# One-hot rows with two steps side by side, and two kinds of products taken in turn, in a graph network stack

## The chip, the cores and the metric

The kernel runs on one core of one Trainium2 chip. The metric is the device time of one execution in microseconds; the kernel before is shown with the median of three runs.

## What is computed

Four graph layers (GCN, graph attention with edge attributes, two GAT convolutions, two SAGE convolutions) run one after another over 3125 nodes with 128 features and 50000 edges. The edges come sorted by their target `dst`. Around each layer there is a layer norm with a relu, and a residual:

```python
edge_index = jnp.stack([src, dst])
h = jnp.maximum(_layernorm(x, axis=-1), 0.0)
x = x + _L0_gnn_ref(h, L0_gnn_W, L0_gnn_b, L0_gnn_gamma, L0_gnn_beta, src, dst)
...
# in _L0_gnn_ref (GCN):
deg_out = jax.ops.segment_sum(ones_e, edge_src, num_segments=N)
norm_out = jax.lax.rsqrt(jnp.maximum(deg_out, 1.0))
h = features * norm_out[:, None]
h = h @ W
agg = jax.ops.segment_sum(h[edge_src], edge_dst, num_segments=N)
```

Only the GCN's sum over edges and the count `deg_out` matter here.

## The kernel before

The sum over edges is done as products with a matrix of counts. Blocks of 128 edges are cut into steps so that one step touches one group of four neighbouring targets; there are STEPS = 1172 steps, taken eight at a time (BATCH = 8) in NB = 147 batches, `b` in the code. Sixteen batches (PER) make a chunk of 128 steps; there are ten chunks (NC). The parts work as follows.

**Histogram.** Before the batches, `hot(turn)` on VectorE (DVE) writes one-hot rows of 16 blocks of edges at a time into `hot_lo` and `hot_hi` (two slots each), and TensorE (PE) multiplies them, 25 columns a product (L1447), to count `deg_out`. There are 25 turns.

**One-hots (L2125, L2127).** For batch `b`, `hot_steps(b)` on DVE compares a constant, `iota_rep`, with the edge's source within its tile (`lo`) and with its key (`key`: source tile and target within the group). This gives `hot_e` (128 x 8) and `hot_k` (KEYS = 100, x 8) of bf16 in one of three slots. The step is the innermost index, so a product of one step reads both with a distance of eight elements, 16 bytes. It signals `hot_done`, and waits for `built` of the batch three back.

**Build products (L1488).** PE multiplies, per step, `hot_e` (weights, 128 x 128) with `hot_k` (100 moving columns) into banks 0 to 3 of PSUM, and signals `built` after the eighth. It waits for `hot_done` of this batch and for `adj_done` of the batch two back.

**Copy.** ScalarE (ACT) copies the eight results as bf16 into `adj` (two chunk slots) and signals `adj_done`.

**SpMM products (L1474).** A finished chunk of `adj` is multiplied with the node rows `xs0` (three bf16 parts and a column of ones, 385 columns): 25 products (one per tile of nodes) make a unit, and there are UNITS = 37 units, in banks 4 to 7. From batch 17 on PE does a quarter of a unit (6 or 7 products) after each batch's build products. The rest comes after the last batch. DVE takes a finished unit out with `v_row` (L2142, L2147).

**What else runs.** From batch 20 on DVE also does `same(g)` (L2135), 98 groups over the remaining batches; each compares `dst_row`, loaded by the SyncE queue (SP) from HBM four groups ahead, and SP stores the result to `same_hbm`. SP also issues zero fills of `starts_q` (one in every second group from g = 10, 28 of them), and the stores of finished chunks to `adj_hbm`. All these are one queue in program order.

When the last unit is done, the rows are picked and summed per node, the GCN's dense part runs, and the three edge passes follow, which take most of the time. They are not touched.

## Time and profile before

| | |
|---|---|
| median of three runs | 2855.87 us (2855.09 to 2861.72) |
| the profiled execution | 2854.37 us |
| its span | 2852.7 us |
| PE, DVE, ACT, POOL busy | 74%, 50%, 34%, 48% of the span |
| build loop (first L2125 to last L1474) | 67.8 to about 455 us |

The span is the time between the first and the last record of the profiled execution; its own time includes what lies around that. Busy shares are means over stages that differ much; the stages of the build loop are looked at one by one below. PE's durations are modelled and overlap, so the distance from one start to the next tells what a product costs. The weight load of a product is shown as PEld.

### The profile page before, as it was taken

Reading aid. Unit: us, or ns where it says so; the run is one execution under the profiler, and the core shown is the slowest. Engines: PE = TensorE matmul, PEld = TensorE weight load, DVE = VectorE, ACT = ScalarE, POOL = GpSimd, SP = SyncE. Lnnn points to the kernel's source line nnn. Section 1 sums busy time; section 2 is a strip of 40 time slices with the busy share of each in tenths; the row PEclk is TensorE's granted clock in tenths of the full one; section 3 lists DMA queues with packets and bytes.
Section 4 is the critical chain, followed back from the end, with each engine's and each line's share of the span. In section 5 each row is a group of like instructions: output and inputs, shape, how many; then the busy total and the mean of one; then the engine's idle time right before and its main releaser. Section 6 shows DMA issues by size and latency. Waiting matters only on the chain.

```text
span 2852.7 us, 33483 instructions
## 1 busy us (share of the span) xinstructions
PE 2108.9 (74%) x10859; PEld 1483.5 (52%) x10859; DVE 1430.3 (50%) x3094; ACT 966.7 (34%) x2148; POOL 1366.6 (48%) x1417
## 2 busy tenths in 40 slices
PE   5899999558888886737777777754444444499998
PEld 4677777247777774523333333443333343266666
DVE  8877673746777665734444444332222222612424
ACT  4533331423333332834444443332222222301202
POOL 3000000667777773577777772457777774300000
PEclk6799999879898886868888887775655555699999
DMA  9599852279999983137777775325555554465461
GB/s 214 171 329 341 310 198 75 81 211 264 265 258 264 269 251 105 27 92 244 240 237 237 244 238 164 84 57 124 138 130 136 132 133 97 165 202 169 130 203 35
DMA packets 518583, 517.97 MB, mean 182 GB/s; under 512 B 153344, under 2 KB 463763, under 8 KB 517227
## 3 DMA queue, kind: packets, MB, share of 16 engines
q1 hardware_dynamic: 310349, 267.63, 30.9%
q0 software_dynamic: 50528, 115.22, 15.9%
q10 hardware_dynamic: 157534, 132.98, 15.1%
q8 instruction: 89, 1.46, 0.2%
q14 instruction: 83, 0.68, 0.1%
HBM read 301.53 MB, written 227.32 MB: 185 GB/s over the span
## 4 chain that ended last, share of the span: by engine, by line
POOL 37%; PE 33%; issue 15%; DVE 9%; DMA 4%; ACT 2%; POOLq 0%; SPq 0%; ACTq 0%; DVEq 0%
POOL arena L1049 34%; PE ps L1586 10%; PE ps L1488 7%; PE ps L1474 5%; PE ps L1568 2%; PE ps L1679 1%; DVE arena L1997 1%; PE ps L1857 1%; DMA arena<-t_attn,src_i 1%; PE ps L1705 1%; DVE arena L2457 1%; DMA arena<-t_gat,src_i 1%; ACT arena L1080 1%; PE ps L1847 1%; POOL starts_q L1000 1%
## 5 line engine op out<-in xcount | busy, mean ns | idle before, releaser
L1080 ACT ACTIVATE arena<-ps 128x774 f32<-128x774 f32 (+8 forms) x689 | 494.4, 730 | 1200.0 <-PE ps L1679 655.1
L1049 POOL DMA_INDIRECT arena<-t_gat,src_i x784 | 740.5, 944 | 239.0 <-issue 236.8
L1679 PE MATMUL ps<-arena 128*128 128x136 f32 (+2 forms) x2352 | 688.5, 454 | 89.6 <-DVE arena L2347 83.0
L1679 PEld LDWEIGHTS ps<-arena 128*128 128x128 f32 x2352 | 462.2, 259 | 238.5 <-DVE arena L2347 114.6
L1049 POOL DMA_INDIRECT arena<-t_attn,src_i x392 | 383.0, 977 | 126.7 <-issue 113.4
L1637 PE MATMUL ps<-ident,logit 128*64 128x128 f32 (+2 forms) x147 | 47.2, 321 | 384.5 <-DVE logit L2308 313.3
L1586 PE MATMUL ps<-arena 128*128 128x384 bf16 x1850 | 306.3, 329 | 33.5 <-DVE rec L2504 31.4
L2295 DVE TENSOR_TENSOR z_b<-arena 128x12 f32<-128x12 f32 (+1 forms) x196 | 34.0, 173 | 587.6 <-DMA arena<-t_gat,src_i 580.4
L1586 PEld LDWEIGHTS ps<-arena 128*128 128x128 bf16 x1850 | 182.3, 99 | 157.2 <-issue 40.2
L1488 PE MATMUL ps<-arena 128*128 128x100 bf16 x1176 | 239.8, 362 | 10.0 <-DVE arena L2127 9.0
L1637 PEld LDWEIGHTS ps<-ident,logit 128*64 128x64 f32 (+2 forms) x147 | 14.1, 96 | 429.4 <-DVE logit L2308 350.3
L2347 DVE TENSOR_TENSOR arena<-arena,ps 128x1536 f32<-128x1536 f32 (+1 forms) x196 | 229.8, 1214 | 1.6 <-ACT arena L1219 1.6
L1008 POOL TENSOR_TENSOR arena<-arena,r_L_gnn_gamma 128x512 f32<-128x512 f32 (+1 forms) x7 | 8.1, 1155 | 456.6 <-ACT arena L1290 456.5
L1488 PEld LDWEIGHTS ps<-arena 128*128 128x128 bf16 x1176 | 169.3, 145 | 59.4 <-DVE arena L2127 13.7
L2287 DVE TENSOR_TENSOR arena<-arena,ps 128x1024 f32<-128x1024 f32 x98 | 119.4, 1218 | 134.4 <-DMA arena<-t_attn,src_i 104.9
L1474 PE MATMUL ps<-arena 128*128 128x385 bf16 x925 | 177.8, 331 | 0.0
L1080 ACT ACTIVATE arena<-same_b 128x512 f32<-128x512 bf16 x294 | 167.7, 621 | 28.0 <-DMA same_b<-same_hbm 28.0
L1080 ACT ACTIVATE arena<-arena 128x512 bf16<-128x512 f32 (+4 forms) x208 | 63.9, 307 | 274.0 <-DVE arena L2600 246.5
L2600 DVE TENSOR_REDUCE arena<-ps 128x128 f32<-128x384 f32 x74 | 36.2, 550 | 220.0 <-PE ps L1586 220.0
L2125 DVE TENSOR_TENSOR arena<-arena 128x1024 bf16<-128x1024 bf16 x147 | 101.7, 692 | 82.1 <-PE ps L1488 81.6
L1474 PEld LDWEIGHTS ps<-arena 128*128 128x128 bf16 x925 | 95.3, 103 | 59.2 <-issue 1.5
L1619 PE MATMUL ps<-w_e,arena 64*128 64x128 f32 x784 | 125.5, 305 | 0.2 <-DVE arena L2287 0.2
(321 smaller groups left out, 2764.1 us busy)
## 6 DMA issues: line engine op xcount, KB each, us to landing
ends_gat<-arena ACTq DMA_DIRECT2D x98, 774.0 KB, 4.1
arena<-adj_hbm SPq DMA_DIRECT2D x90, 640.0 KB, 3.9
same_b<-same_hbm SPq DMA_DIRECT2D x294, 128.0 KB
adj_hbm<-arena SPq DMA_DIRECT2D x9, 3200.0 KB, 12.1
ends_attn<-arena ACTq DMA_DIRECT2D x98, 272.0 KB, 4.8
ends_gat<-arena ACTq DMA_DIRECT2D x98, 258.0 KB, 3.7
arena<-edst SPq DMA_DIRECT2D x98, 256.0 KB, 5.0
starts_q<-zrow SPq DMA_DIRECT2D x28, 896.0 KB, 6.9
```

Of the source, the lines that this page charges most:

```text
L1049: g.indirect_dma_start(out=row_b[:, n % RB, k, 0:row_tab[p].shape[1]], out_offset=None, in_=row_tab[p], in_offset=bass.IndirectOffsetOnAxi ...
L1080: return a.activation(o, i, ACT.Copy)
L1474: i = mm(bank(4 + n % 4)[:, 0:3 * D + 1], lhs, xs0[:, t, 0:3 * D + 1], start=t == 0, stop=t == NT - 1)
L1488: i = mm(ps[:, at:at + KEYS], hot_e[:, b % 3, :, e], hot_k[:, b % 3, :, e], start=True, stop=True)
L1568: i_ = mm(bank(half * 4 + dl)[:, a0 - g0:a1 - g0], l, sel_of[p][:, off + a0:off + a1], start=ch == use[0] and s == 0, stop=ch == use[-1] a ...
L1586: m = mm(bank(ch % 2 * 4 + dl)[:, 0:3 * D], ring[:, u % RING, at:at + P], xs1[:, t, :, :].rearrange("p s c -> p (s c)"), start=t == 0, sto ...
L1619: i = mm(bank((1, 6)[g % 2])[:, k * D:(k + 1) * D], at_t[:, g % 2, k * P:(k + 1) * P], w_e[:, :], start=True, stop=True)
L1637: nc.tensor.transpose(bank(TURN_BANK[p])[0:kh, 0:P], logit[:, i % 2, 0:kh], ident[:, :])\
L1679: i = mm(o, same_f[:, g % RB, k, :], msg[:, g % 4, k * W:(k + 1) * W], start=True, stop=True)
L2125: tt(hot_e[:, b % 3, :, :], iota_rep[:, :, :], bc(lo.rearrange("p (a s) -> p a s", a=1), [P, P, BATCH]), ALU.is_equal)
L2287: tt(kv, kv, bc(bank((1, 6)[g % 2]).rearrange("p (k s c) -> p k s c", k=GC, s=1), [P, GC, 2, D]), ALU.add).then_inc(kve_done.sem, 1)
L2347: tt(m[:, :, 0:heads * nc_].rearrange("p k (h c) -> p k h c", h=heads), rows_v, e, ALU.mult).then_inc(msg_done.sem, 1)
```

## The change

The one-hot tiles get another order: the eight steps of a batch become four pairs, and in each pair the two steps are the innermost index. An element and the next one of the same step are then two elements, 4 bytes, apart. `iota_rep` (128 x 8) becomes `iota_two` (128 x 2), and a filler `room` keeps all tiles behind it where they were. Histogram and batches share one helper, `one_hot`, whose operands have rows of two elements: `iota_two` is read again for each pair, and a pair of `values` is read again for each of the 128 or 100 (or 25) rows. The count of instructions and their sizes on DVE stay, but for the constant.

On PE, `spmm(n, t0, t1)` becomes `product(n, t)`, one product a call. Within a batch one product of the quarter follows each build product as long as there are any (6 or 7), and `built` is signalled by the eighth build product, which now ends the row. ACT's, POOL's and SP's programs are the same.

```diff
@@ -360,14 +360,14 @@
...
-        work = carve(arena, {"iota_rep": (P, (P, BATCH), BF16), "lo_t": (P, (NC, P), BF16), "key_t": (P, (NC, P), BF16),
-                             "hot_e": (P, (3, P, BATCH), BF16), "hot_k": (P, (3, KEYS, BATCH), BF16),
+        work = carve(arena, {"iota_two": (P, (P, 2), BF16), "room": (P, (P * (BATCH - 2) // 2,), F32), "lo_t": (P, (NC, P), BF16), "key_t": (P, (NC, P), BF16),
+                             "hot_e": (P, (3, BATCH // 2, P, 2), BF16), "hot_k": (P, (3, BATCH // 2, KEYS, 2), BF16),
...
-        hists = carve(arena, {"hot_lo": (P, (2, P, WIDE), BF16), "hot_hi": (P, (2, NT, WIDE), BF16)}, hist_at)
+        hists = carve(arena, {"hot_lo": (P, (2, WIDE // 2, P, 2), BF16), "hot_hi": (P, (2, WIDE // 2, NT, 2), BF16)}, hist_at)
@@ -1444,7 +1444,7 @@
...
                 for k in range(n):
-                    i = mm(bank(7)[:, 0:NT], hot_lo[:, slot, :, k], hot_hi[:, slot, :, k],
+                    i = mm(bank(7)[:, 0:NT], hot_lo[:, slot, k // 2, :, k % 2], hot_hi[:, slot, k // 2, :, k % 2],
                            start=turn == 0 and k == 0, stop=turn == HTURNS - 1 and k == n - 1, skip_group_check=True)
@@ -1459,9 +1459,9 @@
...
-            def spmm(n, t0, t1):
+            def product(n, t):
...
-                for t in range(t0, t1):
-                    lhs = adj[:, ch % 2, t * DG + dl, :] if ch < NC - 1 else adj_end[:, t * P:(t + 1) * P]
-                    i = mm(bank(4 + n % 4)[:, 0:3 * D + 1], lhs, xs0[:, t, 0:3 * D + 1], start=t == 0, stop=t == NT - 1)
-                if t1 == NT:
+                lhs = adj[:, ch % 2, t * DG + dl, :] if ch < NC - 1 else adj_end[:, t * P:(t + 1) * P]
+                i = mm(bank(4 + n % 4)[:, 0:3 * D + 1], lhs, xs0[:, t, 0:3 * D + 1], start=t == 0, stop=t == NT - 1)
+                if t == NT - 1:
                     i.then_inc(spmm_done, 1)
...
             def quarter(k):
-                return k % PER_UNIT * NT // PER_UNIT, (k % PER_UNIT + 1) * NT // PER_UNIT
+                return [(k // PER_UNIT, t) for t in range(k % PER_UNIT * NT // PER_UNIT, (k % PER_UNIT + 1) * NT // PER_UNIT)]
...
             for b in range(NB):
                 pe.wait_ge(hot_done, b + 1)
                 if b >= 2:
                     pe.wait_ge(adj_done, b - 1)
+                mixed = quarter(b - PER - 1) if b > PER else []
                 for e in range(BATCH):
                     at = (b % 2 * 2 + e // 4) * BANK + e % 4 * KEYS
-                    i = mm(ps[:, at:at + KEYS], hot_e[:, b % 3, :, e], hot_k[:, b % 3, :, e], start=True, stop=True)
-                i.then_inc(built, 1)
+                    i = mm(ps[:, at:at + KEYS], hot_e[:, b % 3, e // 2, :, e % 2], hot_k[:, b % 3, e // 2, :, e % 2], start=True, stop=True)
+                    if e == BATCH - 1:
+                        i.then_inc(built, 1)
+                    for n, t in mixed[e:e + 1]:
+                        product(n, t)
...
-                if b > PER:
-                    k = b - PER - 1
-                    spmm(k // PER_UNIT, *quarter(k))
@@ -1514,9 +1514,8 @@
...
-                    spmm(n, 0, NT)
-                else:
-                    spmm(n, *quarter(k))
+                for n, t in quarter(k) if n < UNITS - 1 else [(n, t) for t in range(NT)]:
+                    product(n, t)
@@ -1889,7 +1888,7 @@
...
-            v.tensor_copy(iota_rep[:, :, :], bc(iota_i[:, :].rearrange("p (i a) -> p i a", a=1), [P, P, BATCH]))
+            v.tensor_copy(iota_two[:, :, :], bc(iota_i[:, :].rearrange("p (i a) -> p i a", a=1), [P, P, 2]))
@@ -1988,16 +1987,19 @@
...
+            def one_hot(o, parts, values):
+
+                n = o.shape[1]
+                return tt(o, bc(iota_two[:, 0:parts, :].rearrange("p (a i) s -> p a i s", a=1), [P, n, parts, 2]),
+                          bc(values.rearrange("p (a i s) -> p a i s", i=1, s=2), [P, n, parts, 2]), ALU.is_equal)
...
             def hot(turn):
                 slot, at = turn % 2, turn * WIDE
-                r = min(WIDE, CH - at) // BATCH
+                r = min(WIDE, CH - at)
...
                 for o, parts, k in ((hot_lo, P, lo_f), (hot_hi, NT, hi_f)):
-                    i = tt(o[:, slot, :, 0:r * BATCH].rearrange("p i (a k) -> p i a k", a=r),
-                           bc(iota_rep[:, 0:parts, :].rearrange("p i (a k) -> p i a k", a=1), [P, parts, r, BATCH]),
-                           bc(k[:, at:at + r * BATCH].rearrange("p (i a k) -> p i a k", i=1, a=r), [P, parts, r, BATCH]),
-                           ALU.is_equal)
+                    i = one_hot(o[:, slot, 0:r // 2, :, :], parts, k[:, at:at + r])
                 i.then_inc(s_hot, 1)
@@ -2122,10 +2124,8 @@
...
-                tt(hot_e[:, b % 3, :, :], iota_rep[:, :, :], bc(lo.rearrange("p (a s) -> p a s", a=1), [P, P, BATCH]),
-                   ALU.is_equal)
-                tt(hot_k[:, b % 3, :, :], iota_rep[:, 0:KEYS, :],
-                   bc(key.rearrange("p (a s) -> p a s", a=1), [P, KEYS, BATCH]), ALU.is_equal).then_inc(hot_done, 1)
+                one_hot(hot_e[:, b % 3, :, :, :], P, lo)
+                one_hot(hot_k[:, b % 3, :, :, :], KEYS, key).then_inc(hot_done, 1)
```

PE, around batch 17. Before, the first quarters come behind eight build products each (L1456 are transposes of the keys, L1488 build products, L1474 SpMM products):

```order
L1488 MATMUL ps<-arena 128x100 x48
L1456 MATMUL ps<-ident,arena 128x128 x16
L1488 MATMUL ps<-arena 128x100 x96
L1474 MATMUL ps<-arena 128x385 x6
L1488 MATMUL ps<-arena 128x100 x8
L1474 MATMUL ps<-arena 128x385 x6
L1488 MATMUL ps<-arena 128x100 x8
```

Now (L1473 is the SpMM product), from batch 6 on:

```order
L1488 MATMUL ps<-arena 128x100 x89
L1473 MATMUL ps<-arena 128x385
L1488 MATMUL ps<-arena 128x100
L1473 MATMUL ps<-arena 128x385
L1488 MATMUL ps<-arena 128x100
L1473 MATMUL ps<-arena 128x385
L1488 MATMUL ps<-arena 128x100
L1473 MATMUL ps<-arena 128x385
L1488 MATMUL ps<-arena 128x100
L1473 MATMUL ps<-arena 128x385
L1488 MATMUL ps<-arena 128x100
L1473 MATMUL ps<-arena 128x385
```

What moved: the first six SpMM products stand between the build products of batch 17; its last two build products and the first of batch 18 follow in a row.

PE at the end of the build loop, before (the last two batches, then what is left, then the degrees, L1502):

```order
L1474 MATMUL ps<-arena 128x385 x7
L1488 MATMUL ps<-arena 128x100 x8
L1474 MATMUL ps<-arena 128x385 x6
L1488 MATMUL ps<-arena 128x100 x8
L1474 MATMUL ps<-arena 128x385 x94
```

Now:

```order
L1473 MATMUL ps<-arena 128x385
L1488 MATMUL ps<-arena 128x100
L1473 MATMUL ps<-arena 128x385
L1488 MATMUL ps<-arena 128x100
L1473 MATMUL ps<-arena 128x385
L1488 MATMUL ps<-arena 128x100 x2
L1473 MATMUL ps<-arena 128x385 x88
L1502 MATMUL ps<-arena,vdeg 4x128
```

What moved: the last batch's quarter lies between its build products, and 88 products are left in one row, before 94.

## Rows read from the trace of the kernel before

**Rows 1.** The page: the span, and each engine's busy time, share and instructions.

```profile
span 2852.7 us, 33483 instructions
...
PE 2108.9 (74%) x10859; PEld 1483.5 (52%) x10859; DVE 1430.3 (50%) x3094; ACT 966.7 (34%) x2148; POOL 1366.6 (48%) x1417
```

**Rows 2.** Stages in us: busy time (instructions) by engine, granted clock, DMA share, GB/s.

```profile
27.00:62.00 35.00, 28.10 (x375) 25.77 (x376) 34.97 (x52) 25.97 (x120) 23.75 (x21) 0.50 1.18 278
...
67.80:105.00 37.20, 28.71 (x140) 20.38 (x141) 32.91 (x70) 24.25 (x48) 0.00 (x0) 0.55 0.69 175
105.00:114.70 9.70, 8.62 (x42) 5.54 (x40) 8.03 (x17) 3.98 (x6) 0.00 (x0) 0.51 0.01 2
114.70:147.70 33.00, 33.00 (x189) 23.93 (x188) 22.93 (x44) 10.88 (x13) 0.00 (x0) 1.00 0.63 219
147.70:329.10 181.40, 181.40 (x1036) 130.97 (x1034) 133.99 (x264) 60.59 (x73) 0.00 (x0) 1.00 0.97 343
329.10:427.80 98.70, 98.70 (x564) 71.19 (x563) 71.11 (x132) 33.49 (x40) 0.00 (x0) 1.00 0.62 214
427.80:455.00 27.20, 27.20 (x167) 16.76 (x166) 10.29 (x36) 2.51 (x3) 0.00 (x0) 1.00 0.38 157
```

**Rows 3.** Waits from 105 to 455 us: who for whom, total us, times, longest.

```profile
DVE arena L2125 <- PE ps L1488: 81.6, 114, 1.7
...
DVE same_b L2135 <- DMA arena<-edst: 5.0, 3, 2.6
```

**Rows 4.** Timeline of one batch: start, duration (us), engine, line, count, idle before.

```profile
249.86 1.41 PEld L1488 LDWEIGHTS ps<-arena 128*128 128x128 bf16 x8
...
251.31 0.95 PEld L1474 LDWEIGHTS ps<-arena 128*128 128x128 bf16 x6
...
252.34 1.39 PEld L1488 LDWEIGHTS ps<-arena 128*128 128x128 bf16 x8
252.50 1.61 PE L1488 MATMUL ps<-arena 128*128 128x100 bf16 x8
```

**Rows 5.** Timeline: one batch's build products while the granted clock is 0.50.

```profile
71.35 1.68 PE L1488 MATMUL ps<-arena 128*128 128x100 bf16 x8 [0.56 <-DVE arena L2127]
```

**Rows 6.** Timeline of PE near the program's end, products of bf16 rows.

```profile
2633.30 6.43 PE L1568 MATMUL ps<-arena 128*128 128x121 bf16 x63
```

**Rows 7.** Groups by shape in that stretch, seven in all: busy us, mean ns.

```profile
L1568 PE MATMUL ps<-arena 128*128 128x391 bf16 x9 | 2.0, 331 | 0.0
...
L1568 PE MATMUL ps<-arena 128*128 128x20 bf16 x12 | 0.9, 173 | 0.0
```

**Rows 8.** Timeline of DVE in the histogram.

```profile
27.02 26.96 DVE L1997 TENSOR_TENSOR arena<-arena 128x2048 bf16<-128x2048 bf16 x38
```

**Rows 9.** Two lines of DVE: duration ns min/median/max, first and last start, shapes.

```profile
L2125 DVE TENSOR_TENSOR arena<-arena x147: 670/694/696, 67.8 to 426.7; 128x1024 bf16<-128x1024 bf16 x147
...
L2033 DVE TENSOR_TENSOR arena<-arena x2: 427/822/1216, 64.7 to 73.5; 128x256 int32<-128x256 int32 x1, 128x1024 int32<-128x1024 int32 x1
```

**Rows 10.** L2125 alone by stage: its busy us and (x) its instructions.

```profile
147.70:329.10 181.40, 49.89 (x72) 1.00 0.97 343
329.10:427.80 98.70, 27.77 (x40) 1.00 0.62 214
```

**Rows 11.** DMA issues of 147.7:329.1, then 329.1:427.8: KB each, us to landing.

```profile
starts_q<-zrow SPq DMA_DIRECT2D x28, 896.0 KB, 6.9
...
arena<-edst SPq DMA_DIRECT2D x55, 256.0 KB, 5.6
...
arena<-edst SPq DMA_DIRECT2D x29, 256.0 KB, 4.1
```

**Rows 12.** Timeline of the end of the build loop.

```profile
427.33 0.57 DVE L2127 TENSOR_TENSOR arena<-arena 128x800 bf16<-128x800 bf16 x1
...
432.46 1.39 PEld L1488 LDWEIGHTS ps<-arena 128*128 128x128 bf16 x8
...
433.88 15.48 PEld L1474 LDWEIGHTS ps<-arena 128*128 128x128 bf16 x94
```

More of the change, by code:

```diff
@@ L362, in gnn_stack_kernel @@
         cmp, val_i, val_f = (look[k] for k in ("cmp", "val_i", "val_f"))
-        work = carve(arena, {"iota_rep": (P, (P, BATCH), BF16), "lo_t": (P, (NC, P), BF16), "key_t": (P, (NC, P), BF16),
-                             "hot_e": (P, (3, P, BATCH), BF16), "hot_k": (P, (3, KEYS, BATCH), BF16),
+        work = carve(arena, {"iota_two": (P, (P, 2), BF16), "room": (P, (P * (BATCH - 2) // 2,), F32), "lo_t": (P, (NC, P), BF16), "key_t": (P, (NC, P), BF16),
+                             "hot_e": (P, (3, BATCH // 2, P, 2), BF16), "hot_k": (P, (3, BATCH // 2, KEYS, 2), BF16),
                              "dst_row": (P, (UNROLL, GC, P), I32)}, work_at)
-        iota_rep, lo_t, key_t, hot_e, hot_k, dst_row = (
-            work[k] for k in ("iota_rep", "lo_t", "key_t", "hot_e", "hot_k", "dst_row"))
+        iota_two, lo_t, key_t, hot_e, hot_k, dst_row = (
+            work[k] for k in ("iota_two", "lo_t", "key_t", "hot_e", "hot_k", "dst_row"))
         block_i = dst_row[:, 0, :, :].rearrange("p k e -> p (k e)")[:, 0:CH]
         hist_at = work_at + P * BATCH // 2 + NC * P
-        hists = carve(arena, {"hot_lo": (P, (2, P, WIDE), BF16), "hot_hi": (P, (2, NT, WIDE), BF16)}, hist_at)
+        hists = carve(arena, {"hot_lo": (P, (2, WIDE // 2, P, 2), BF16), "hot_hi": (P, (2, WIDE // 2, NT, 2), BF16)}, hist_at)
         hot_lo, hot_hi = hists["hot_lo"], hists["hot_hi"]
@@ L1460, in _ @@
             keys_of(0, SOON, 0, 1)
-            def spmm(n, t0, t1):
+            def product(n, t):
                 ch, dl = n // DG, n % DG
-                if t0 == 0:
+                if t == 0:
                     pe.wait_ge(adj_done, min(NB, (ch + 1) * PER))
```

## The prediction

> **What bounds the kernel now.** I read the page first, for the whole, and then the table by stage, because the change touches only the first 455 us. Over the span PE is busy 74% and no engine is full [rows 1]; that average says nothing here. The table by stage [rows 2] does: from 114.7 to 455 us PE has no idle time at all, at a granted clock of 1.00, while DVE is busy 23 of 33, 134 of 181 and 71 of 99 us. The waits agree: DVE waits 81.6 us in 114 pieces for the build products of L1488, and only 5.0 us for a DMA [rows 3]. So in this stretch the build loop runs at PE's pace. All that follows waits for its end, so what it saves counts in full.
>
> What does PE do in a batch? The timeline of one batch in the steady part [rows 4] gives it: eight weight loads of L1488 begin at 249.86, six of L1474 at 251.31, and the next eight at 252.34. A batch takes 2.48 us. The eight build products take 1.45 us, 181 ns each; the six products of L1474 take 1.03 us.
>
> 181 ns is far too much for 100 moving columns. Late in the program products of the same type, with rows that lie together in memory, do 63 matmuls in 6.4 us [rows 6]. Their columns go from 391 down to 20 in seven shapes (391, 377, 276, 249, 148, 121, 20, mean 226) [rows 7]: 102 ns each, 0.45 ns a column. 100 columns at that rate are 45 ns. For a product of 385 columns I use 165 ns, from the 94 in a row in 15.48 us [rows 12]. So a build product loses some 136 ns, and the loss isn't the array's: at a granted clock of 0.50 the eight take 1.68 us [rows 5], at 1.00 1.61 us [rows 4]. The array's clock halves and the time stays. What is left is the read of the operands, which both step over 16 bytes from one element to the next.
>
> **The change part by part.** *Reading (L1488).* Elements now lie 4 bytes apart. The trace has no such read, so I bound it: 181 ns if every element still costs the same, 45 ns if the operand is read as rows that lie together. I take 45, since the neighbours that share 16 bytes are four instead of one, and 181/4 = 45 too. The Trainium skill ("SBUF — State Buffer", section "Door 1: The DMA port swizzle") says that SBUF has lines of 16 bytes, and that two hits on a line are enough for full speed. By that rule four hits give the 45 ns; by the upper bound nothing is gained and the sum is 0. The exact price matters little: any up to about 100 ns serves, as the rivals show.
>
> *Order.* Build products and L1473 products (L1474 before) alternate one by one. A weight load goes on beside the product before it [rows 4], so I cost the alternation at nothing: 6.25 products of 165 ns cover 6 of 8 build loads. `built` now comes at the end of the mixed row and not 1 us before it, but ACT's copy (its result is wanted two batches on) has a batch to hide in, and DVE waits for a batch three back. If a load were not covered, it would cost 6 times some 50 ns a batch, and PE would still not be the bound. A batch on PE is then 8 x 0.045 + 6.25 x 0.165 = 1.39 us.
>
> *DVE.* The one-hots write the same number of elements, in rows of two. The pair (L2125, L2127) takes 694 ns for 1024 elements, against 1216 ns for 1024 at one a cycle (L2033) [rows 9]: it runs in pairs now. Bounds: 694 if pairs go on, 1216 if not. I take 694, as the innermost step stays one element and two elements still lie together. The constant `iota_two` is a quarter of `iota_rep`; that is work before the first load has landed, worth nothing.
>
> *Next bound, by stage.* After PE comes what is second in each row of rows 2. A batch count per stage is in [rows 10]: 72 and 40 in the two long ones (13 in the one before).
> - Up to 67.8 us: the 25 turns of the histogram (L1447) run at the pace of DVE, which makes 38 one-hots in 26.96 us without a gap [rows 8]. Saved: 0.
> - 67.8 to 114.7: DVE is busy 32.9 of 37.2 and 8.0 of 9.7 us; of the 6 idle us about a third is PE's builds. Saved: 2.
> - 114.7 to 147.7: DVE 22.9 us, DMA 0.63 x 33 = 20.8. DVE binds, with some waits as a 3200 KB store runs ahead of the loads: 25 for 33. Saved: 8.
> - 147.7 to 329.1: DVE 134 us, but DMA is busy 0.97 x 181.4 = 176 us. All 28 zero fills [rows 11] and the first groups of `same` lie here. The share is a true ceiling, for the bytes per busy time are the same when it is low: 219/0.63 = 348 GB/s, 343/0.97 = 354, 214/0.62 = 345 [rows 2]. DVE can still run ahead once: loads of `dst_row` are issued four groups ahead, 4 x 3.24 = 13 us, and land in 5.6 us (4.1 in the lighter stage) [rows 11]. So the queue may grow by 7 us: between 169 and 178, I take 173. Saved: 8.
> - 329.1 to 427.8: DVE 71.1; DMA 61.2 and the 7 us left over. Both near 70; I take 76, since the `adj` stores are bunched. Saved: 23.
> - 427.8 to 455: DVE's last pair ends at 427.9, yet PE begins the last batch only at 432.46 and ends its builds at 433.9 [rows 12]. That lag of 4.6 us goes, and 1.1 of the builds. Saved: 6. The 87 products and the final 25 after it stay.
>
> Sum: 0 + 2 + 8 + 8 + 23 + 6 = 47. The profiled execution took 2854.4 us (span 2852.7), 1.5 us under the median of the three runs, 2855.9. 2854.4 - 47 = 2807.4, so 2809 for the median.
>
> **The rivals.** *DMA is no ceiling* (0.07). The share counts packets in flight, and a deeper queue moves more. Then the long stage falls to DVE's 134 us, the next to 71: 93 us saved in all, 2763. For it: the share is 1.18 from 27 to 62 us, at 278 GB/s [rows 2]. Against it: bytes per busy us do not move with the load.
>
> *The read gains nothing* (0.04): the cost is per element, not per 16 bytes. PE keeps 2.48 us and the time is 2856. It decides from 100 ns a product: above it PE's batch passes DVE's 134/72 = 1.84 us.
>
> *DVE loses its pairs* (0.11), which ends on the other side. The rows of two are too short, or `values` reads the same two elements 128 times. At 1216 ns the pair of one-hots costs 0.94 us more a batch. DVE's batch is then 1.84 + 0.94 = 2.78 us against 2.48: 0.30 x 127 = 38. The first 17 batches, at DVE's pace now, cost 17. The histogram pays 0.53 for each 1024 elements, 1.27 us x 25 = 32. Less 6 for the lag: 81 slower, 2937. It decides at about half of that: with 0.47 a batch DVE stays under 2.48, the gain of the stages (20) and the loss of the first batches and the histogram (8 and 16) cancel, 2860. For it: no row shows rows of two. Against it: L2125 reads eight elements again and again now and holds its pairs.
>
> The Trainium skill speaks on both sides of this. "Vector Engine (DVE) Microarchitecture Reference", section "5.1 Performance modes — why throughput varies by op and dtype", asks for 16-bit elements, an innermost step of one and more than one element in it, which holds here. Section 5.2, "Measured stream behaviour on trn2", says a port keeps its rate only in runs of two or more adjacent 4-byte words; `values` now has runs of one word. The trace of before has no such read, so it can't say which applies to a word that is read again; by the second page the half-way case above would come true, 2860.
>
> **How the numbers follow.** The forecast has 0.78, with a range of its own from 2795 to 2830: +-5 for the DMA's ceiling, +-5 for bunched stores, +-5 for DVE's waits. The range 2785 to 2850 leaves out the rival without a ceiling (0.07), the one without a gain (0.04), most of the DVE one (0.08). A measurement of this kernel can tell about 0.3% from no change, 8.6 us. Faster: 0.78 + 0.07 less a little = 0.84. Same: 0.04 + 0.03 = 0.07. Slower: 0.09, the DVE rival and what I have not seen.
>
> **What would show it.** Weight loads of L1488 some 100 ns long or less, and PE idle in the build loop, waiting for DVE; DVE waiting for `dst_row` between 150 and 320 us, with a DMA share of 0.97 or more there and landings of 9 us or more; DVE busy nearly all of the time after it; L1993 at 694 and 570 ns; the last L1473 product near 408 us. Wrong would be: L1993 above 900 ns; PE without idle time; or no wait of DVE for a DMA, which makes it faster than I say. Behind the build loop the trace should be the old one, shifted.

## The result

The changed kernel takes 2830.6 us in the median of four runs (2821.6 to 2839.5), the kernel before 2856.7: a ratio of 0.9907, with a 95% interval from 0.9892 to 0.9922. That is 26 us faster; 47 were forecast. The profiled execution is the slowest of the four, 2839.5 us. Its page answers to [rows 1]:

```profile
span 2837.8 us, 33483 instructions
...
PE 1970.9 (69%) x10859; PEld 1366.4 (48%) x10859; DVE 1421.0 (50%) x3094; ACT 966.4 (34%) x2148; POOL 1389.4 (49%) x1417
```

**The build loop.** The table by stage, cut at the same events as [rows 2] (first one-hot of a batch, groups 0, 10, 66 and the end of the groups, last SpMM product), which now come at other times (the first cut, 98.40, lies 0.2 us behind the loop's first one-hot, which starts at 98.2):

```profile
98.40:144.50 46.10, 23.40 (x196) 17.73 (x197) 41.01 (x85) 27.96 (x53) 0.00 (x0) 0.74 0.09 25
144.50:171.10 26.60, 21.05 (x189) 14.09 (x187) 21.89 (x43) 10.88 (x13) 0.00 (x0) 0.87 0.75 267
171.10:336.00 164.90, 116.50 (x1042) 75.67 (x1040) 128.86 (x264) 62.24 (x75) 0.00 (x0) 0.92 1.03 379
336.00:413.50 77.50, 65.39 (x571) 43.34 (x572) 67.83 (x132) 32.64 (x39) 0.00 (x0) 0.88 0.77 270
413.50:435.00 21.50, 21.50 (x140) 12.57 (x139) 10.09 (x35) 1.67 (x2) 0.00 (x0) 1.00 0.48 199
```

PE has idle time in every stage but the last. The stages took 33.0, 181.4, 98.7 and 27.2 us and take 26.6, 164.9, 77.5 and 21.5. From the loop's first one-hot to its last SpMM product it was 387 us (67.8 to 455) and is 337 (98.2 to 435): 50 us less. The waits from 130 to 435 us say who binds now, beside [rows 3]; then the durations of the two lines of the change, beside [rows 4, 9], and four products in the middle of the loop:

```profile
DVE same_b L2135 <- DMA arena<-edst: 49.7, 15, 7.6
...
DVE arena L1993 <- PE ps L1488: 2.4, 3, 0.9
```

```profile
L1488 PEld LDWEIGHTS ps<-arena x1176: 97/98/153, 99.5 to 414.7; 128*128 128x128 bf16 x196
...
L1993 DVE TENSOR_TENSOR arena<-arena x344: 258/622/1223, 32.3 to 412.8; 128x1024 bf16<-128x1024 bf16 x148, 128x2048 bf16<-128x2048 bf16 x24
```

```profile
253.35 0.21 PE L1488 MATMUL ps<-arena 128*128 128x100 bf16 x1
253.40 0.33 PE L1473 MATMUL ps<-arena 128*128 128x385 bf16 x1
253.56 0.21 PE L1488 MATMUL ps<-arena 128*128 128x100 bf16 x1
253.61 0.33 PE L1473 MATMUL ps<-arena 128*128 128x385 bf16 x1
```

A pair of products takes 0.21 us, start to start, of which the SpMM product alone is 165 ns. DVE keeps its pairs: 2048 elements in at most 1223 ns, 0.6 ns each, where L2033 needs 1.19 [rows 9].

**Ahead of the loop.** The loop begins at 98.2 us, where it began at 67.8. These 30.4 us are the whole of what is missing, and more. 5.3 us of them are a first load that landed later in this execution; the histogram starts at 32.3 and not at 27.02 [rows 8]. The rest shows on POOL, which gathers the edges of the steps (`es`, L978, and `ed`, L981, two for each chunk, 20 in a row) while DVE makes the histogram's one-hots. First the timeline of POOL before, then after:

```profile
26.48 1.14 POOL L978 DMA_INDIRECT arena<-esrc,step_i  x1 [21.79 <-DMA edst<-pad_i]
27.93 2.83 POOL L981 DMA_INDIRECT arena<-edst,step_i  x1 [0.31 <-issue]
31.05 1.13 POOL L978 DMA_INDIRECT arena<-esrc,step_i  x1 [0.30 <-issue]
```

```profile
31.68 1.23 POOL L978 DMA_INDIRECT arena<-esrc,step_i  x1 [26.99 <-DVE step_i L1981]
33.22 26.84 POOL L981 DMA_INDIRECT arena<-edst,step_i  x1 [0.30 <-issue]
60.37 1.26 POOL L978 DMA_INDIRECT arena<-esrc,step_i  x1 [0.31 <-issue]
```

The second gather took 2.83 us and takes 26.84. Nobody else is late there: DVE's histogram runs at its old pace. DVE then needs the gathered edges, and the waits from 26 to 130 us name it:

```profile
DVE arena L2025 <- DMA arena<-edst,step_i: 25.4, 1, 25.4
```

The long gather ends at 60.06 us, only behind turn 18 of the histogram (59.23), where DVE does two small operations (a reciprocal and a product) before turn 19. What differs on DVE ahead of that? Its timeline at turns 1 and 2, before:

```profile
28.15 1.50 DVE L1997 TENSOR_TENSOR arena<-arena 128x400 bf16<-128x400 bf16 x2
28.43 1.50 DVE L1997 TENSOR_TENSOR arena<-arena 128x2048 bf16<-128x2048 bf16 x2
29.56 1.53 DVE L1997 TENSOR_TENSOR arena<-arena 128x400 bf16<-128x400 bf16 x2
29.87 1.50 DVE L1997 TENSOR_TENSOR arena<-arena 128x2048 bf16<-128x2048 bf16 x2
```

and after:

```profile
33.45 0.36 DVE L1993 TENSOR_TENSOR arena<-arena 128x400 bf16<-128x400 bf16 x1
33.72 1.22 DVE L1993 TENSOR_TENSOR arena<-arena 128x2048 bf16<-128x2048 bf16 x1
34.86 0.36 DVE L1993 TENSOR_TENSOR arena<-arena 128x400 bf16<-128x400 bf16 x1
35.14 1.22 DVE L1993 TENSOR_TENSOR arena<-arena 128x2048 bf16<-128x2048 bf16 x1
```

From a row of 400 to the next row of 2048 it is 0.28 us, but once before it was 0.31. At turn 2 DVE waits for PE to free the slot of turn 0, and PE, which needed 64 ns a product, was some 30 ns late. Now PE's 16 products take 0.6 us, DVE never waits, and its row has no gap until turn 18.

The theory from this (**POOL shut out**): while DVE's one-hots follow each other without a gap, POOL cannot finish a gather. Rivals: the long gather has nothing to do with DVE (**chance**), or the new rows of two keep POOL out whenever they run (**rows of two**).

### The profile page after: what moved, and what is told of

It reads as the page before. It is cut to its first block, busy times and chain, and to the rows that moved or that the text cites. A ratio compares the mean times of both kernels' runs of the same rounds, so it can differ in the third digit from the quotient of the medians.

```text
span 2837.8 us, 33483 instructions
## 1 busy us (share of the span) xinstructions
PE 1970.9 (69%) x10859; PEld 1366.4 (48%) x10859; DVE 1421.0 (50%) x3094; ACT 966.4 (34%) x2148; POOL 1389.4 (49%) x1417
## 3 DMA queue, kind: packets, MB, share of 16 engines
q1 hardware_dynamic: 310349, 267.63, 30.8%
## 4 chain that ended last, share of the span: by engine, by line
POOL 41%; PE 21%; issue 16%; DVE 11%; DMA 7%; ACT 2%; SPq 1%; POOLq 0%; ACTq 0%; DVEq 0%
POOL arena L1049 37%; PE ps L1585 10%; DMA arena<-edst 4%; DVE arena L1993 3%; PE ps L1567 2%; PE ps L1473 1%; POOL arena L981 1%; PE ps L1856 1%; DVE same_b L2135 1%; PE ps L1678 1%; PE ps L1704 1%; DVE arena L2457 1%; ACT arena L1080 1%; PE ps L1846 1%; ACT arena L1290 1%
## 5 line engine op out<-in xcount | busy, mean ns | idle before, releaser
L1488 PE MATMUL ps<-arena 128*128 128x100 bf16 x1176 | 212.4, 223 | 88.9 <-DVE arena L1993 87.5
L1585 PEld LDWEIGHTS ps<-arena 128*128 128x128 bf16 x1850 | 182.8, 99 | 158.3 <-issue 41.6
L1473 PE MATMUL ps<-arena 128*128 128x385 bf16 x925 | 219.2, 343 | 0.5 <-ACT arena L1080 0.5
L1993 DVE TENSOR_TENSOR arena<-arena 128x1024 bf16<-128x1024 bf16 (+1 forms) x344 | 205.0, 648 | 2.9 <-PE ps L1488 2.4
L1488 PEld LDWEIGHTS ps<-arena 128*128 128x128 bf16 x1176 | 113.3, 106 | 112.6 <-DVE arena L1993 101.7
L1473 PEld LDWEIGHTS ps<-arena 128*128 128x128 bf16 x925 | 93.6, 101 | 60.8 <-issue 12.7
```

The lines of the kernel that those rows point to most:

```text
L1473: i = mm(bank(4 + n % 4)[:, 0:3 * D + 1], lhs, xs0[:, t, 0:3 * D + 1], start=t == 0, stop=t == NT - 1)
L1488: i = mm(ps[:, at:at + KEYS], hot_e[:, b % 3, e // 2, :, e % 2], hot_k[:, b % 3, e // 2, :, e % 2], start=True, stop=True)
L1585: m = mm(bank(ch % 2 * 4 + dl)[:, 0:3 * D], ring[:, u % RING, at:at + P], xs1[:, t, :, :].rearrange("p s c -> p (s c)"), start=t == 0, sto ...
L1993: return tt(o, bc(iota_two[:, 0:parts, :].rearrange("p (a i) s -> p a i s", a=1), [P, n, parts, 2]), bc(values.rearrange("p (a i s) -> p a ...
```

## The experiments

### One gap more, and one gap less

**A pause in the changed kernel.** DVE waits at turn 2 for PE's turn 1, which has just been given out:

```diff
...
                 if turn >= 2:
-                    dve.wait_ge(s_hist, turn - 1)
+                    dve.wait_ge(s_hist, 2 if turn == 2 else turn - 1)
...
```

> The changed kernel, but at turn 2 of the histogram DVE waits until PE has multiplied turn 1, not turn 0: one pause of DVE of about half a microsecond. Theory (POOL shut out): in the changed kernel DVE's one-hots of the histogram follow each other without any gap, and the second row gather of POOL (L981) took 26.8 us because of it; one pause is enough to let it through. Then the second gather takes under 5 us, the first batch starts near 73 us and not near 98, and the time is about 25 us under the changed kernel's: 2806, against 2831. Rival 1 (the long gather was a delay of DMA or memory that has nothing to do with DVE): no difference, 2831. Rival 2 (rows of two read SBUF so often that POOL is kept out whenever such an operation runs): the pause lets one gather through and the next is kept out until turn 18, the first batch again near 98 us, 2831.

Measured: 2808.2 us (2805.5 to 2811.5), ratio 0.9838 (0.9821 to 0.9854). DVE's row, and POOL's:

```profile
29.08 2.91 DVE L1993 TENSOR_TENSOR arena<-arena 128x2048 bf16<-128x2048 bf16 x4
32.73 8.29 DVE L1993 TENSOR_TENSOR arena<-arena 128x2048 bf16<-128x2048 bf16 x11 [0.74 <-PE ps L1447]
```

```profile
29.99 2.83 POOL L981 DMA_INDIRECT arena<-edst,step_i  x1 [0.31 <-issue]
33.12 1.65 POOL L978 DMA_INDIRECT arena<-esrc,step_i  x1 [0.30 <-issue]
```

One pause of 0.74 us saves 22. The gather ends 0.1 us behind the pause, and of the other 18 all but two (1.65 and 1.55 us) then go by in 1.1 us each, most of them beside the same one-hots. So chance and rows of two both fall. The first build product is at 71.5 us, and from there to the last SpMM product it is 335 us, as in the changed kernel (99.5 to 434.8).

**The old histogram under the new batches.** `hot_lo` and `hot_hi` and their one-hots as before, the rest as changed.

```diff
...
-                    i = mm(bank(7)[:, 0:NT], hot_lo[:, slot, k // 2, :, k % 2], hot_hi[:, slot, k // 2, :, k % 2],
+                    i = mm(bank(7)[:, 0:NT], hot_lo[:, slot, :, k], hot_hi[:, slot, :, k],
...
```

> The changed kernel with the histogram's one-hots in the old layout (16 steps innermost, PE reads every 32 bytes); the batches keep the new one. PE's histogram products are slow again, about 64 ns, so DVE waits once for PE at turn 2. Theory (POOL shut out) and rival 2 (rows of two): the second gather takes under 5 us, first batch near 70 us, time 2806. Rival 1 (a delay that has nothing to do with DVE): 2831. The build loop should be as in the changed kernel, 337 us from its first one-hot to its last SpMM product.

Measured: 2808.0 us, ratio 0.9836 (0.9820 to 0.9852). No gather takes over 1.9 us. So PE's slow histogram was what helped POOL: at turn 2 the gap between DVE's starts is 0.02 us longer again.

**The kernel before with a third slot**, so that DVE waits for a turn three back. This takes the gap away and leaves every layout alone; the third slot is a tile of its own.

```diff
...
-                slot, at = turn % 2, turn * WIDE
+                slot, at = turn % 3, turn * WIDE
...
-                if turn >= 2:
-                    dve.wait_ge(s_hist, turn - 1)
+                if turn >= 3:
+                    dve.wait_ge(s_hist, turn - 2)
...
```

> The kernel before with a third slot for the histogram's one-hots, so that DVE never waits for PE there; nothing else is changed, the old layout stays. Theory (POOL shut out by the lack of a gap): the second gather is kept out for over 20 us, as in the changed kernel, the first batch starts near 93 us and not near 68, and the time is 25 us above the kernel before: 2881. Rivals 1 and 2: the kernel before, 2856.

Measured: 2877.5 us, ratio 1.0082 (1.0065 to 1.0098). A slot more makes the old kernel 22 us slower. POOL:

```profile
26.59 1.23 POOL L979 DMA_INDIRECT arena<-esrc,step_i  x1 [21.89 <-DMA edst<-pad_i]
28.12 26.84 POOL L982 DMA_INDIRECT arena<-edst,step_i  x1 [0.31 <-issue]
```

**The new histogram alone** in the kernel before, with nothing of the change in the batches:

```diff
...
-        hists = carve(arena, {"hot_lo": (P, (2, P, WIDE), BF16), "hot_hi": (P, (2, NT, WIDE), BF16)}, hist_at)
+        hists = carve(arena, {"hot_lo": (P, (2, WIDE // 2, P, 2), BF16), "hot_hi": (P, (2, WIDE // 2, NT, 2), BF16)}, hist_at)
...
```

> The kernel before with the histogram alone in the new layout; batches and order are the old ones. Theory (POOL shut out) and rival 2: the second gather takes over 20 us, the first batch starts near 93 us, the time is 25 us above the kernel before, 2881. Rival 1: 2856. PE's products in the histogram should follow each other at 27 ns and not at 64.

Measured: 2882.5 us, ratio 1.0104 (1.0077 to 1.0131). Here the first gather is the one that is held, 27.12 us. PE's 16 products of a turn take 0.65 us. This part of the change costs 27 us by itself and gains nothing. PE's granted clock does not go with the hold either: over the histogram it was 0.50 here and 1.00 in the changed kernel and with the third slot, where a gather was held too; it was 0.50 in the kernel before and 1.00 with the pause, where none was held beyond turn 2.

### When the pause comes

The changed kernel, with its one pause at turn 8 and not at turn 2:

```diff
...
                 if turn >= 2:
-                    dve.wait_ge(s_hist, turn - 1)
+                    dve.wait_ge(s_hist, 8 if turn == 8 else turn - 1)
...
```

> The changed kernel, with DVE's one pause at turn 8 of the histogram (it waits there for PE's turn 7) and not at turn 2. Theory (one gap in DVE's row lets POOL's gather through, and the gather is held until there is one): the gather that was held ends with the pause, about 8 turns of 1.41 us = 11.3 us behind the histogram's start. So it takes 8 to 12 us: less than 26.8 (gap at turn 18), more than 2.8 (gap at turn 2). The first batch starts some 7 us later than with the pause at turn 2, where its first build product was at 71.6 us: 78. Time 2808 + 7 = 2815. If the gap were not what frees it, but only how early in the histogram it lies: as the changed kernel, 2831.

Measured: 2811.0 us, ratio 0.9849 (0.9832 to 0.9865). The gather is held until the pause, here too:

```profile
27.50 11.38 DVE L1993 TENSOR_TENSOR arena<-arena 128x2048 bf16<-128x2048 bf16 x16
39.59 11.11 DVE L1993 TENSOR_TENSOR arena<-arena 128x2048 bf16<-128x2048 bf16 x15 [0.72 <-PE ps L1447]
```

```profile
27.55 12.30 POOL L978 DMA_INDIRECT arena<-esrc,step_i  x1 [22.86 <-DMA edst<-pad_i]
```

27.55 + 12.30 = 39.85, against DVE's restart at 39.59. With gaps at turns 2, 8 and 18 the held gather takes 2.8, 12.3 and 26.8 us. The first build product is 6.0 us later than with the pause at turn 2 (77.5), as expected; the time is only 3 us longer, where 7 were expected, and the two ratios' intervals overlap.

### What is held

For the histogram alone the constant becomes f32, once in PSUM (the diff) and once in a tile of the same shape in SBUF; there is no pause. All else is the changed kernel.

```diff
...
+        iota_wide = bank(5)[:, 0:2 * P].rearrange("p (i s) -> p i s", s=2)
...
-                    i = one_hot(o[:, slot, 0:r // 2, :, :], parts, k[:, at:at + r])
+                    i = one_hot(o[:, slot, 0:r // 2, :, :], parts, k[:, at:at + r], iota_wide)
...
```

> The changed kernel, without a pause; for the histogram alone the constant is f32 and lies in PSUM, so that DVE's one-hots read one operand from SBUF and not two. They should be slower, one element a cycle: 2048 elements some 2.2 us and not 1.2, the histogram some 68 us and not 35, and DVE's row is again without a gap. Theory (DVE holds a way into SBUF that POOL needs, and only because it reads both operands there): no gather takes over 5 us. If it is any row of DVE instructions without a gap: a gather of over 40 us, until turn 18 (18 x 2.7). Time if it is let through: 2808 + 33 = 2841; if not: 2860.

> The twin of the run with the constant in PSUM: the same f32 constant, in SBUF. The histogram is as slow as there. Theory (two operands in SBUF hold POOL out, at one element a cycle too): a gather of over 40 us, until turn 18; time 2860. If only DVE's fast mode (two elements a cycle) holds POOL out: no gather over 5 us, 2841.

Measured, one execution each: 2839.6 us in PSUM, 2856.3 in SBUF. DVE, then POOL, with the constant in PSUM:

```profile
27.27 50.98 DVE L1995 TENSOR_TENSOR arena<-ps,arena 128x2048 bf16<-128x2048 f32 x38
```

```profile
26.89 1.11 POOL L979 DMA_INDIRECT arena<-esrc,step_i  x1 [22.19 <-DMA edst<-pad_i]
28.30 0.95 POOL L982 DMA_INDIRECT arena<-edst,step_i  x1 [0.30 <-issue]
29.56 0.95 POOL L979 DMA_INDIRECT arena<-esrc,step_i  x1 [0.30 <-issue]
```

and in SBUF:

```profile
26.81 51.15 DVE L1995 TENSOR_TENSOR arena<-iota_f,arena 128x2048 bf16<-128x2048 f32 x38
```

```profile
28.88 50.06 POOL L979 DMA_INDIRECT arena<-esrc,step_i  x1 [24.19 <-DMA edst<-pad_i]
79.25 2.18 POOL L982 DMA_INDIRECT arena<-edst,step_i  x1 [0.31 <-issue]
81.73 2.37 POOL L979 DMA_INDIRECT arena<-esrc,step_i  x1 [0.30 <-issue]
```

DVE's row is equally long (51 us for 38) and equally gapless in both. With one operand in PSUM the gathers take 0.95 us, as long as the last ones of its twin, when the histogram is over. With both in SBUF one is held for 50 us. So it is not a gapless row as such, nor the two elements a cycle, but the second operand that DVE reads in SBUF. The reading rests on the traces, each a single one; the two times differ by 17 us, the way that the theory has it. The granted clock over the histogram differed too (0.50 with PSUM, 1.00 with SBUF), but the runs above show holds at either.

The starts show one thing more. Beside DVE's rows the gathers that come after the gap start 1.41 us apart (31.05, 32.49, 33.91 in the kernel before), which is one turn of DVE, and in the SBUF run 2.69 us apart (79.25, 81.73, 84.41, 87.10), which is one turn of its slower DVE. With the operand in PSUM they start 1.25 us apart, their own 0.95 and the 0.30 of issue. So they still feel DVE: they have fallen in step with its turns. Why a gather can fall in step only after a gap is open.

The Trainium skill ("SBUF — State Buffer", section "Who interferes with whom") says that DVE and GpSimd share a pair of ports under an exclusive lock, and that a DVE instruction with two inputs in SBUF contends with a GpSimd instruction that reads SBUF. The traces agree as far as the second operand goes (50.06 us with it, 0.95 without), and these gathers read their indices from a tile in SBUF (`step_i`); no port shows in them. The same section infers that a `tensor_tensor`, which these one-hots are, does not hold up the writing of a DMA's descriptors; here it held up an indirect DMA for 26.84 us, and the measurement decides. By the Trainium skill's figure (the same page, section "A bandwidth-pool intuition that's wrong (but worth ruling out)") a blocked DMA goes on about 115 ns behind the end of DVE's instruction; here the ends of nearly all of 38 instructions in a row let the held gather go on no further.

### The order

```diff
...
-                    for n, t in mixed[e:e + 1]:
-                        product(n, t)
...
+                for n, t in mixed:
+                    product(n, t)
...
```

> The pause at turn 2, the new layout, but PE's order as before: eight build products, then the six or seven SpMM products. It measures the alternation. By the prediction (its cost and its worth are nothing, since DVE and DMA bound the loop): 2808, the same as with the alternation, within 0.3%. The rival: eight weight loads of 98 ns in a row are not covered by matmuls of 46 ns, a build product costs 98 ns and PE needs 0.8 + 1.03 = 1.8 us a batch; that is as much as DVE's 1.84, and the loop loses some us: 2812 to 2820.

With the pause, the new layout and PE's old order it takes 2804.9 us, ratio 0.9824 (0.9808 to 0.9841): the same as with the alternation (0.9838), rather below than above it. Eight new build products in a row follow each other at 45 to 52 ns, so a weight load that reads 98 ns long is covered by matmuls of about 50.

The alternation alone in the kernel before:

```diff
...
                 for e in range(BATCH):
...
+                    for n, t in mixed[e:e + 1]:
+                        product(n, t)
...
```

> The kernel before with the alternating order alone; all one-hots keep the old layout. PE's work a batch stays 8 x 181 + 6.25 x 165 ns = 2.48 us, so the loop keeps PE's pace. By the prediction: 2856, the same within 0.3%, perhaps 1 us less at the loop's end. The rival, that alternating hides a part of a build product's slow read beside the product before it: PE's batch falls under 2.48 us, the stretch from group 10 to group 97 under the 280 us of before, the time under 2845.

Measured: 2853.1 us, ratio 0.9983 (0.9974 to 0.9993). A pair of products, start to start, takes 0.34 us:

```profile
251.03 0.35 PE L1473 MATMUL ps<-arena 128*128 128x385 bf16 x1
251.22 0.34 PE L1488 MATMUL ps<-arena 128*128 128x100 bf16 x1
251.37 0.35 PE L1473 MATMUL ps<-arena 128*128 128x385 bf16 x1
```

0.345 - 0.165 = 0.18 us for the build product, as in a row of them. Alternating hides next to nothing of the slow read. It is not worth quite nothing, though: the whole interval lies under 1, the median is 4.6 us lower, and with PE's first build product at 69.1 us in both the last SpMM product starts at 451.1 us, where it started at 455.1. 3.0 of these 4.0 us are there when the last build product starts (433.9 and 430.9), some 23 ns in each of about 130 batches; the last 1.0 is the row of 88 products in place of 94 (6 x 0.165).

### The price of the read

Four steps side by side in place of two, in the batches and in the histogram, so that one step's elements lie 8 bytes apart; the pause at turn 2 is kept.

```diff
...
-                    i = mm(ps[:, at:at + KEYS], hot_e[:, b % 3, e // 2, :, e % 2], hot_k[:, b % 3, e // 2, :, e % 2], start=True, stop=True)
+                    i = mm(ps[:, at:at + KEYS], hot_e[:, b % 3, e // 4, :, e % 4], hot_k[:, b % 3, e // 4, :, e % 4], start=True, stop=True)
...
```

> The pause at turn 2, with four steps side by side and not two: PE reads with a distance of 8 bytes, so two elements of a step lie in 16 bytes. It prices the read. If the cost goes by pieces of 16 bytes touched (181 ns at one element in each, 46 at four), a build product costs some 90 ns; PE then needs 8 x 0.09 + 1.03 = 1.75 us a batch, still under DVE's 1.84, and the time is 2808 to 2812. If two elements in 16 bytes are enough for full speed: 46 ns a product, the same as at 4 bytes. One-hots on DVE keep 694 ns, and the time is 2808.

Measured: 2809.9 us, ratio 0.9840 (0.9823 to 0.9856). PE in the middle of the loop:

```profile
251.49 0.25 PE L1488 MATMUL ps<-arena 128*128 128x100 bf16 x1
251.56 0.35 PE L1473 MATMUL ps<-arena 128*128 128x385 bf16 x1
251.74 0.25 PE L1488 MATMUL ps<-arena 128*128 128x100 bf16 x1
```

A pair takes 0.256 us over many. Less the 165 ns of the SpMM product, 100 columns cost 180, 91 and 44 ns at a distance of 16, 8 and 4 bytes: it doubles with the distance, and two elements in 16 bytes are not enough for full speed. Without the alternation's help: eight in a row at 8 bytes follow each other at 94 ns.

### The ceiling behind PE

Half of the zero fills come behind the loop (pause at turn 2 kept):

```diff
...
-                if g >= 10 and g % 2 == 0 and g // 2 - 5 < ZERO_PARTS:
-                    zeros(starts["attn"], ZERO_PARTS, g // 2 - 5, 256)
+                if g >= 10 and (g - 10) % 6 == 0 and (g - 10) // 6 < ZERO_PARTS // 2:
+                    zeros(starts["attn"], ZERO_PARTS, (g - 10) // 6, 256)
...
+            for at in range(ZERO_PARTS // 2, ZERO_PARTS):
+                zeros(starts["attn"], ZERO_PARTS, at, 256)
...
```

> The pause at turn 2, and half of the zero fills of starts_q (14 of 28, 896 KB each) behind the last SpMM product, where the DMA engines are nearly idle (share 0.10 from 406.8 to 450 us); the other 14 are spread over the loop, one in six groups. It tests the ceiling of the prediction: with the pause alone the groups from g = 10 to g = 97 take 242.9 us, while DVE is busy 205 of them. If the DMA engines bind there, 14 fills of 2.5 us less leave about 202 us of DMA work against DVE's 205, and the stretch falls to some 210 us: time 2808 - 33 = 2775. If DMA is no ceiling and DVE's waits have another cause: 2808. If the late fills hold up what comes behind (POOL waits for all fills before it begins at 452.6 us): over 2780 although the stretch is short.

Measured: 2794.0 us, ratio 0.9791 (0.9771 to 0.9812). From group 10 to 66 and from there to 97, first with the pause alone, then with half of the fills later:

```profile
142.40:307.70 165.30, 116.47 (x1042) 75.62 (x1039) 128.96 (x264) 62.25 (x75) 0.00 (x0) 0.93 1.03 377
307.70:385.30 77.60, 64.82 (x570) 42.95 (x570) 67.83 (x132) 32.65 (x39) 0.00 (x0) 0.88 0.77 273
```

```profile
141.40:290.20 148.80, 115.49 (x1032) 75.22 (x1029) 128.27 (x264) 61.41 (x74) 0.00 (x0) 0.95 0.89 316
290.20:368.50 78.30, 64.65 (x570) 43.04 (x570) 67.82 (x132) 32.64 (x39) 0.00 (x0) 0.88 0.86 301
```

The fills did cost time: the first stretch loses 16.5 us. The edit takes them both off the DMA engines and out of SP's queue, where they ran ahead of loads of `dst_row`, and this run doesn't tell the two apart. That the engines were full in the changed kernel is argued from their share, 1.00 to 1.09 in each piece of 16 or 17 us from 188 to 336 us. And 33 us were expected: the stretch stops at 148.8 with a share of 0.89 and DVE busy 128. Over both stretches DVE still waits 30.8 us for `dst_row`, in 8 waits. So the big stores are cut, with the half of the fills still behind the loop:

```diff
...
-                if kept < NC - 1 and g == groups_by((kept + 1) * PER + 3):
-                    store_adj(kept)
-                    kept += 1
+                part = g - groups_by((kept + 1) * PER + 3)
+                if kept < NC - 1 and 0 <= part < 4:
+                    store_adj(kept, part)
+                    kept += part == 3
...
```

> As with half of the fills later, and each of the first eight 3200 KB stores of adj is cut in four of 800 KB, issued at four groups in a row. With half of the fills later, the groups from g = 10 to g = 97 took 227.1 us, and DVE still waited 30.8 us for dst_row, in 8 waits, the longest 5.6 us. If these waits are the big stores standing ahead of a load of dst_row in the queue, they shrink to under 10 us, the stretch falls to some 208 us, near DVE's 205, and the time to 2794 - 18 = 2776. If they are the DMA engines' total work, nothing changes: 2794.

Measured: 2777.2 us (2773.5 to 2781.7), ratio 0.9714 (0.9701 to 0.9728), the fastest of all. The same stretches:

```profile
142.20:277.80 135.60, 112.81 (x1043) 73.37 (x1041) 128.50 (x265) 61.41 (x74) 0.00 (x0) 1.00 0.95 333
277.80:357.10 79.30, 61.53 (x546) 40.09 (x545) 68.09 (x132) 31.81 (x38) 0.00 (x0) 0.94 0.90 321
```

The first falls by 13 us, to 7 above DVE's busy time, where DVE waits 7.1 us for `dst_row`, at most 1.3 at a time; the longer waits there were for a load behind a store of 3200 KB. What cut stores gain with all of the fills in the loop was not tried, so the 13 us can't be carried over to the changed kernel. The second doesn't fall; 12.2 us of waits for `dst_row` stay there, with one of 4.0. What holds them was not tried (the two fills of `starts_er` lie there).

## Why the prediction was right or wrong

The time, 2830.6, lies in the range, 22 us above the 2809 forecast. That it does is owed to the width of the range: nothing in the prediction foresaw these 22 us. The kernels that let POOL through, but are else the changed one, take 2808. So the sum came out but for one step; within it the long stage gave twice its term, and the terms around it a little less than theirs.

- **The step that failed** is "Up to 67.8 us ... Saved: 0". That DVE sets the histogram's pace is true (38 one-hots in 26.9 to 27.0 us wherever the constant is bf16 and no pause is put in). But I looked only at who waits for whom between DVE and PE, and costed a faster PE at nothing. PE's lateness of 30 ns was the only gap in which POOL's gather got through. Measured price: 22 us (with and without the pause, 2808.2 against 2830.6), 22 (a third slot), 27 (the new histogram alone); the stage up to the first one-hot, costed at 0, became 30.4 us longer in the profiled execution, 5.3 of them the late load. No rival had it; the one on the slower side, DVE losing its pairs, would have cost 81 and did not come.
- **The read** was forecast at 45 ns and costs 44. The reason that I gave (four neighbours in 16 bytes, 181/4) fits: 180, 91 and 44 ns for one, two and four of them. No run shows the 16 bytes as such, since no build product stepped over more. By the Trainium skill's rule ("SBUF — State Buffer", section "Door 1: The DMA port swizzle", lines of 16 bytes, two hits suffice) the forecast would be the same at 4 bytes, but at 8 bytes it gives 45 where 91 are measured; the measurement decides.
- **DVE keeps its pairs**: a 128x2048 one-hot takes 1.22 us in either layout. Of the two sections of the Trainium skill weighed ("Vector Engine (DVE) Microarchitecture Reference"), 5.1 on performance modes agrees with this; by 5.2 the half-way case would have come, and it did not for a word that is read again.
- **The order** was costed at nothing. In the old layout it saves 4.6 us (ratio 0.9983, interval under 1), in the new one it saves nothing: without it the median is 3 us lower, and the intervals overlap.
- **The stages**, in us saved, named by their times before and measured in the profile of after:

  | stage | forecast | measured |
  |---|---|---|
  | 67.8 to 114.7 | 2 | under 1 (46.9 and 46.3) |
  | 114.7 to 147.7 | 8 | 6.4 |
  | 147.7 to 329.1 | 8 | 16.5 |
  | 329.1 to 427.8 | 23 | 21.2 |
  | 427.8 to 455 | 6 | 5.7 |
  | in sum | 47 | 50 |

  The long stage was mis-sized most: I held 354 GB/s a busy microsecond for a ceiling, and the engines now move 379 at a share of 1.03, 368. "DMA is no ceiling" falls all the same: that stage did not fall to DVE's 134 us (164.9, with 36.0 us of waits for `dst_row`), and moving fills away shortens it.
- **Waits for `dst_row`** came as foretold (49.7 us from 5.0), with PE idle in the loop; the landings of 9 us or more did not (median 6.4 us in the long stage); the last L1473 product, foretold near 408 us, is at 435.0, and at 406.8 with the pause.
- In the profiled execution the loop ends 20 us earlier (435.0 against 455.0), and the span is 14.9 us shorter. The other 5 us came behind the loop, in code that did not change; with the pause that part is as long as before (2397.0 and 2397.7 us), so I don't ascribe them to the change.

## What to carry to other kernels

When a change makes an engine faster, also look for gaps that its slowness made in another engine's row, and for who used them: here 30 ns of PE's lateness were worth 22 us to POOL. If GpSimd has to issue DMAs while DVE works through a row of operations with both operands in SBUF, give that row a pause early on (one was enough). One operand in PSUM lets the DMAs through as well, but here it was an f32 one and made the row 51 us long in place of 27, so that the kernel took 2839.6 us and not 2808; a PSUM operand at full speed was not tried. In a matmul's strided read, count the bytes stepped over: at 4 bytes a column costs what it does in rows that lie together (0.44 against 0.45 ns), and at 8 and 16 the price doubles each time.

## What the runs showed of the hardware that was not expected

- GpSimd's indirect DMA can be held for a whole row of DVE instructions, not only for one: 26.8 us over nearly all of the 38 one-hots up to turn 18, 50.1 us over the same at half speed. A gap of some 30 ns (0.304 in place of 0.277 us from one start to the next, which the third slot took away) was enough to end it. The held gather ended 0.8 to 1.0 us behind the start of the gap or the end of the row (0.83 with the pause at turn 2, 0.98 at turn 8, 0.83 in the changed kernel, 0.98 with f32 in SBUF), about what a gather takes with nobody beside it (0.94). Afterwards gathers of 1.1 us went on beside the same row without another gap, one in each turn of DVE.
- With one of DVE's operands in PSUM the same gathers took 0.95 us, but for the first (1.11), and came at their own pace of 1.25 us.
- A build product costs 0.44, 0.91 and 1.80 ns a column where its operands step over 4, 8 and 16 bytes. At 16 bytes that is the same at a granted clock of 0.50 and of 1.00 ([rows 4, 5]); at 4 bytes products in a row follow each other at 82 ns at 0.50 (125 to 138 us of the changed kernel) and at 45 to 52 where it is mostly 1.00 (old order, from 150 us on). From 99 to 112 us of the changed kernel they take 82 ns too, though the granted clock reads 1.00 there; that stays open. Weights and moving operand step alike in all of these runs, so the two were not told apart.
